# Cross-attention context: V as the stationary operand on two 64-column halves of the array, with the softmax denominators summed by ScalarE and spread by small DMAs

## The reference, cut to what matters

```python
xn = layernorm(layernorm(x)) * ln_gamma + ln_beta               # 8 batches x 256 tokens x 128
q = (xn @ w_q).reshape(B, 256, 16, 64)
k, v = split(context @ w_kv)                                    # 512 keys x 16 heads x 64
scores = einsum('bqhd,bkhd->bhqk', q * SCALE, k)
attn = softmax(scores, axis=-1)
out = einsum('bhqk,bkhd->bqhd', attn, v).reshape(B, 256, 1024)
x = x + tanh(g_xattn) * tanh(gate) * (out @ w_out + b_out)
x = x + tanh(g_ffn) * switch_ffn(layernorm(x))                  # 8 experts, 160 rows each
```

## Time and profile before

| | before |
|---|---|
| time, median of 3 (lowest to highest) | 473.65 us (472.65 to 474.98) |
| profiled execution, span from first to last instruction | 473.7 us |
| busy: PE, DVE, ACT, POOL | 439.7, 360.3, 386.4, 356.6 us |
| share of 16 DMA engines' span in the packets of SP's queue | 93.4% |
| granted TensorE clock, mean | 0.996 |
| first to last DMA transpose | 23.7 to 427.1 us |

### The profile page before, as it was taken

How to read it: one execution, slowest core, us unless ns; L and a number is a source line. 1 busy time by engine, 2 the same in 40 slices (tenths; PEclk the granted TensorE clock), 3 DMA queues, 4 the chain that set the end, 5 groups by cost and what they waited for, 6 DMA issues and landing times.

```text
span 473.7 us, 13155 instructions
## 1 busy us (share of the span) xinstructions
PE 439.7 (93%) x5096; PEld 334.0 (71%) x5096; DVE 360.3 (76%) x789; ACT 386.4 (82%) x630; POOL 356.6 (75%) x270
## 2 busy tenths in 40 slices
PE   7889799998999989999999999999999999988993
PEld 6656667776767767776777667776777677758892
DVE  4787687778877887779787796878877887785622
ACT  5889788899888988899888898899799998892330
POOL 3687686888788887888878877898878877871325
PEclk9999999999999999999999999999999999999998
DMA  5499999999999999999999999999989998996021
GB/s 167 150 177 192 206 187 175 170 181 204 188 176 188 210 194 180 192 192 192 198 189 197 189 196 191 185 200 209 190 157 185 193 180 147 159 182 137 14 67 46
DMA packets 283037, 82.10 MB, mean 173 GB/s; under 512 B 264387, under 2 KB 280435, under 8 KB 282976
## 3 DMA queue, kind: packets, MB, share of 16 engines
q1 hardware_dynamic: 281600, 77.96, 93.4%
q0 software_dynamic: 1376, 3.30, 2.2%
HBM read 10.83 MB, written 5.14 MB: 34 GB/s over the span
## 4 chain that ended last, share of the span: by engine, by line
PE 40%; DVE 20%; ACT 16%; DMA 10%; issue 8%; POOL 4%; POOLq 0%; SPq 0%; ACTq 0%; DVEq 0%
DVE MXL L903 9%; DMA PT<-PARTS 9%; ACT P L752 7%; DVE HL L890 4%; ACT HL L714 4%; PE psAB L1234 3%; PE psX L1319 3%; PE psAB L1241 3%; PE psO L1267 3%; ACT PARTS L762 3%; POOL PARTS L650 3%; PE psX L1355 3%; DVE VL L896 3%; PE psO L1269 3%; PE psO L1268 3%
## 5 line engine op out<-in xcount | busy, mean ns | idle before, releaser
L650 POOL TENSOR_TENSOR PARTS<-P,PARTS 128x1024 f16<-128x1024 f32 x125 | 267.4, 2145 | 63.5 <-ACT PARTS L762 61.8
L762 ACT ACTIVATE PARTS<-P 128x1024 f16<-128x1024 f32 x126 | 136.1, 1080 | 0.7
L752 ACT ACTIVATE P<-psAB,NB 128x512 f32<-128x512 f32 x128 | 81.6, 695 | 41.8 <-DVE NB L906 41.4
L903 DVE TENSOR_REDUCE MXL<-psAB 128x2 f32<-128x1024 f32 x64 | 78.4, 1224 | 41.4 <-PE psAB L1241 23.9
L1267 PE MATMUL psO<-VH,PT 128*128 128x65 f16 x1008 | 98.6, 194 | 8.3 <-DMA PT<-PARTS 7.7
L1267 PEld LDWEIGHTS psO<-VH,PT 128*128 128x128 f16 x1008 | 92.0, 98 | 12.0 <-DMA PT<-PARTS 8.9
L1268 PE MATMUL psO<-VL,PT 128*128 128x64 f16 x1008 | 98.5, 192 | 0.0
L1269 PE MATMUL psO<-VH,PT 128*128 128x65 f16 x1008 | 98.4, 193 | 0.0
L1268 PEld LDWEIGHTS psO<-VL,PT 128*128 128x128 f16 x1008 | 91.3, 98 | 0.5
L1269 PEld LDWEIGHTS psO<-VH,PT 128*128 128x128 f16 x1008 | 91.5, 97 | 0.0
L752 ACT ACTIVATE P<-psCD,NB 128x512 f32<-128x512 f32 x128 | 81.7, 703 | 0.1
(11 more groups left out here) (214 smaller groups left out, 871.7 us busy)
## 6 DMA issues: line engine op xcount, KB each, us to landing
ctx_raw<-in_ctx_dram SPq DMA_DIRECT2D x8, 256.0 KB, 3.7
w1s<-in_L_ffn_w_dram SPq DMA_DIRECT2D x8, 256.0 KB, 3.6
w2s<-in_L_ffn_w_dram SPq DMA_DIRECT2D x8, 256.0 KB, 4.0
PT<-PARTS SPq DMA_TRANSPOSE x126, 5.0
experts_table<-zeros POOLq DMA_DIRECT2D x2, 645.0 KB, 4.0
X<-in_x_dram SPq DMA_DIRECT2D x8, 128.0 KB, 4.2
wraw<-in_L_xattn_w_kv_dram SPq DMA_DIRECT2D x4, 256.0 KB, 5.3
out_dram<-row SPq DMA_DIRECT2D x8, 128.0 KB, 2.5
```

Source lines behind the costliest of these rows:

```text
L650: pool.tensor_tensor(PARTS[:, par, qt, 1], P32[:, par, qt], PARTS[:, par, qt, 0], ALU.subtract).then_inc(plo_done, 1)
L752: last = act.activation(P32[:, par, qt, SK * h:SK * h + SK], score_bank(qt)[:, SK * h:SK * h + SK], ACT.Exp, bias=NB[:, par, qt, h:h + 1])
L762: act.activation(PARTS[:, hp % 2, qt, 0], P32[:, hp % 2, qt], ACT.Copy).then_inc(phi_done[qt], 1)
L903: dve.tensor_reduce(MXL[:, par, qt, :, 0], score_bank(qt)[:].rearrange("p (h n) -> p h n", h=2), AX.X, ALU.max, negate=True).then_inc(max_ ...
```

## The change

V becomes the stationary operand. For each key tile and each of the three products, head 0's V (128 keys x 64) sits on the first 64 columns of the array and head 1's on the other 64, and PT moves with 256 columns (both query tiles). That makes 24 matmuls for each pair instead of 48; psO[0:64] and psO[64:128] hold the two heads' context with the queries along the row. It is already the layout of OT, so `o_transposes`, `ot_copy`, the tensor O and their semaphores go. The sums of the exponentials no longer come out of the matmul: `exps` writes them by ScalarE's accumulator output into `den`. They lie there with the queries on the partitions, while OT needs them along the row, so DVE's `recips` takes reciprocals into `rden`, SP stores these 512 numbers one by one into a DRAM buffer (`recips_store`) and loads each head's 256 numbers back into 64 partitions (`recips_load`, two DMAs). Only the last pair goes another way: a copy on POOL, two PE transposes and a copy on ACT.

```diff
+    recip_rows = nc.dram_tensor("recip_rows", (2, 2, SQ), F32).ap()
@@ sync
+            def recips_store(j):
+                par = j % 2
+                sp.wait_ge(rden_done, j + 1)
+                if j >= 2:
+                    sp.wait_ge(recips_in, 32 * (j - 1))
+                sp.dma_start(recip_rows[par].rearrange("h (t p) -> p h t", p=P), rden[:, par],
+                             allow_slow_non_contiguous=True).then_inc(recips_out, 16)
+            def recips_load(j):
+                par = j % 2
+                sp.wait_ge(recips_out, 16 * (j + 1))
+                if j >= 2:
+                    sp.wait_ge(norm_done, j - 1)
+                for h in range(2):
+                    sp.dma_start(rdenT[DH * h:DH * h + DH, par, :], recip_rows[par, h:h + 1, :].to_broadcast([DH, SQ]))\
+                        .then_inc(recips_in, 16)
...
                     if j < LAST:
-                        for qt in range(QT):
-                            transpose_parts(j, qt)
+                        transpose_parts(j, 0)
+                        recips_store(j)
+                        transpose_parts(j, 1)
+                        recips_load(j)
@@ scalar
-            def ot_copy(n, bank=psOT, pairs=1):
...
+            def recip_copy():
...
                     last = act.activation(P32[:, par, qt, SK * h:SK * h + SK], score_bank(qt)[:, SK * h:SK * h + SK],
-                                          ACT.Exp, bias=NB[:, par, qt, h:h + 1])
+                                          ACT.Exp, bias=NB[:, par, qt, h:h + 1], accum_out=den[:, par, h, qt:qt + 1])
@@ vector
+            def recips(j):
+                par = j % 2
+                dve.wait_ge(exp_done, 2 * j + 2)
+                if j >= 2:
+                    dve.wait_ge(recips_out, 16 * (j - 1))
+                dve.reciprocal(rden[:, par], den[:, par]).then_inc(rden_done, 1)
...
             def normalise_heads(b, hp):
...
-                dve.reciprocal(rden[:, hp % 2, :], sums[:, :, DH]).then_inc(rden_done, 1)
...
+                    dve.wait_ge(recips_in, 32 * (j + 1))
...
+                dve.tensor_tensor(OT[:, hp, :], psO[:, 0:SQ], rdenT[:, hp % 2, :], ALU.mult).then_inc(norm_done, 1)
...
                     row_max(b, hp, 0)
+                    if j:
+                        recips(j - 1)
@@ tensor
-                            pe.matmul(psO[:, g:g + DH + 1], phi, VH[:, kt, head, 0:DH + 1], start=first_, stop=False)
-                            pe.matmul(psO[:, g:g + DH], phi, VL[:, kt, head, :], start=False, stop=False)
-                            last = pe.matmul(psO[:, g:g + DH + 1], plo, VH[:, kt, head, 0:DH + 1], start=False,
-                                             stop=last_)
+                pt = PTL[:] if j == LAST else PT[:, par]
+                for kt in range(KT):
+                    for v, s in ((VH, 0), (VH, 1), (VL, 0)):
+                        for h in range(2):
+                            last = pe.matmul(psO[DH * h:DH * h + DH, 0:SQ], v[:, kt, 2 * hp + h, :], pt[:, :, s, h, kt, :],
+                                             start=(kt == 0 and v is VH and s == 0),
+                                             stop=(kt == KT - 1 and v is VL))
...
-            def o_transposes(n, bank=psOT, pairs=1):
...
+            def spread_recips():
```

More of the change, by code:

```diff
@@ L258, in gated_block @@
         rden_done = sem("rden_done")
+        recips_out = sem("recips_out")
+        recips_in = sem("recips_in")
+        recip_spread = sem("recip_spread")
+        recip_psum = sem("recip_psum")
+        recip_copied = sem("recip_copied")
         norm_done = sem("norm_done")
-        ot_psum = sem("ot_psum")
-        ot_done = sem("ot_done")
         proj_psum = sem("proj_psum")
@@ L731, in router_exp @@
                 last.then_inc(lexp_done, 1)
-            def ot_copy(n, bank=psOT, pairs=1):
[L735 to L742, removed]
+            def recip_copy():
+                act.wait_ge(recip_psum, 1)
+                act.wait_ge(norm_done, LAST - 1)
+                act.activation(rdenT[:, LAST % 2, :], psRT, ACT.Copy).then_inc(recip_copied, 1)
             def exps(b, hp, qt):
@@ L1070, in batch @@
                         place(B - 2)
+                        recips(LAST)
                     if hp == LOGITS_STEP and is_last(b):
@@ L1314, in project_part @@
                     wait_x((part_done, b + 1))
-                pe.wait_ge(ot_done, b * PAIRS + pairs[-1] + 1)
+                pe.wait_ge(norm_done, b * PAIRS + pairs[-1] + 1)
                 pe.wait_ge(wo_in, 16)
@@ L1318, in project_part @@
                     for pair in pairs:
-                        last = pe.matmul(bank[:, D * qt:D * qt + D], OT[:, pair * QT + qt, :], wo[:, pair, :],
+                        last = pe.matmul(bank[:, D * qt:D * qt + D], OT[:, pair, P * qt:P * qt + P], wo[:, pair, :],
                                          start=(pair == pairs[0]), stop=(pair == pairs[-1]))
@@ L1344, in project_last @@
                     for pair in pairs:
-                        last = pe.matmul(dst, OT[:, pair * QT + qt, :], wo[:, pair, :], start=(pair == pairs[0]),
+                        last = pe.matmul(dst, OT[:, pair, P * qt:P * qt + P], wo[:, pair, :], start=(pair == pairs[0]),
                                          stop=(pair == pairs[-1]))
@@ L1354, in project @@
                     for pair in range(PAIRS // 2, PAIRS):
-                        last = pe.matmul(dst, OT[:, pair * QT + qt, :], wo[:, pair, :], start=(pair == PAIRS // 2),
+                        last = pe.matmul(dst, OT[:, pair, P * qt:P * qt + P], wo[:, pair, :], start=(pair == PAIRS // 2),
                                          stop=(pair == PAIRS - 1))
@@ L1399, in batch @@
                         q_project(*next_pair(b, hp, AHEAD))
-                    if ot_pair(j) >= 0:
-                        if not ahead:
-                            pe.wait_ge(kq_done, LAST + 1)
-                            pe.wait_ge(ot_done, ot_pair(j))
-                        o_transposes(ot_pair(j))
                     if hp == RANKS_STEP and b > 1:
```

78 lines of the change are left out of this document (27 added, 51 removed).

## The result

The changed kernel takes **973.13 us** (967.79 to 974.95, 4 runs) against 474.15 us of the kernel before (472.65 to 474.98, 4 runs) on the same chip: a ratio of 2.048, 95% interval 2.042 to 2.054. The forecast was 530, with 485 to 600 as its range. The sign was right and the size was far off: 499 us were added, not 56.

What follows compares the result with a forecast made beforehand. SP's ordered DMA list was taken to bound the changed kernel, 7.4 us a pair against a period of 6.45; 62 x 0.95 = 59, less 1 for start and end, on 473.7 gave 531.7, rounded to 530 us, range 485 to 600.

Steps and rivals of the forecast that it cites:

- What bounds the kernel: SP's ordered DMA list: 5.6 us of a 6.45 us pair before, 0.85 to spare; 7.4 after the change, 0.95 over.
- The issue of the new DMAs: On SP's queue, each pair: 0.58 us for the store, 1.05 for two loads, 0.15 for further waits and steps.
- The store waits for `rden_done`: SP's store waits for DVE's reciprocals, which stand behind the next pair's first maximum: taken as 0, up to 0.3 us.
- the store's landing: SP's loads wait for it: 2.5 us against 3.1 of issues between, so wait 0; upper bound 4.6, a 1.5 us wait.
- The late-store rival: Single numbers into DRAM land as late as scattered rows, 4.6 us: 625 us, or 590 at 1 us of wait; chance 0.13.
- a sixth of 5 us: DMA packets: 512 + 128 more beside two transposes' 4,096 add at most 0.8 us a pair, 0.4 of it in spare time.
- The ring through VectorE: DVE standing at the multiplication for `recips_in` would hold up the next maximum; put at nothing.
- The column halves overlap: PE's values matmuls on two column halves run together: 1.44 us a pair, not 2.88, making PE 0.24 us a pair shorter.
- Start and end: Outside the pairs: O's last transposes and ACT copy (0.49 + 0.61 us) leave, the last loads join; counted as -1 us.
- No overlap: Rival: PE's column halves run in series, PE gets 1.2 us a pair longer, period 7.65, time 548 us; chance 0.15.
- Packets only: Rival: SP's issue time is pushed back, not spent, so only the packets' time counts: 498 us; chance 0.10.
- Faster: Rival: SP's list does not bind, PE and ACT do, 0.24 and 0.41 us less; 458 us with PE's share; chance 0.08.

Runs made afterwards that it cites:

- the loads alone: Changed kernel with only the first two pairs' stores kept; every pair's two loads stay and later ones reread those old numbers: 547.17 us, ratio 1.154.
- the run with the store alone: Changed kernel with each pair's store of 512 single numbers but without the reciprocal loads, a constant standing in rdenT: 810.78 us, ratio 1.707.
- the run without DMAs: Changed kernel without the store and two loads of the reciprocals, constants in their place except for the last pair: 483.04 us, ratio 1.017.
- the run with 16-byte runs: Changed kernel with all its DMAs, but the store writes each partition's four numbers side by side, 128 runs of 16 bytes (wrong scales): 563.09 us, ratio 1.182.

## Why the prediction was wrong in size

- **What bounds the kernel: right.** SP's ordered list had little to spare: between the issues of the kernel before lie 55.5 us, 0.89 a pair, where 0.85 and 0.15 were taken. With the loads alone its timeline has hardly a gap. What that list costs when it is full was taken too low (below).
- **The issue of the new DMAs: right in the changed kernel, too low in a full list.** 0.534 us for the store (0.58 taken), 1.09 for most pairs of loads (1.05 taken), but there SP had stood for 6.6 us (416.3 / 63) before the loads. Where it issues without a pause, two loads take 1.4 us.
- **The store waits for `rden_done`, taken as 0: right.** It waited once, 1.5 us.
- **The failed step: the store's landing.** It was taken from the row store at 2.5 us, with the scattered DMA's 4.6 us as the upper bound. It is 9.3 us, twice the bound. Runs of 512 bytes were a row for a DMA of as many runs, but no row had single numbers side by side, and that is what costs: the same 512 numbers 64 bytes apart landed in 2.9 us. The late-store rival named the place and put 4.6 us at its end, so the range ended at 600 and that rival at 625 (its case of a wait of 1 us works out to 594, not 590, and the 555 of both waits to 556; nothing rests on either).
- **A step that was missing: what the store does to others.** Late landing was priced as a wait of SP. By the run with the store alone, the store costs 328 us over the run without DMAs with nobody waiting for its landing in the same pair. Transposes behind it land in 10.3 to 11.3 us in place of 5.0. The estimate of "a sixth of 5 us" for the added packets took all packets for equally long. The ring through VectorE, put at nothing, stayed small in the changed kernel (11.4 us of waiting for the loads at the product), but it is what took the gain when the loads came a pair later.
- **The sum with the failed step mended** is the run with 16-byte runs: a period of (513.1 - 24.1) / 62.5 = 7.82 us and 563.09 us, against 7.4 and 530. SP's queue in it, us a pair between the first and the last transpose:

| | taken | 16-byte runs |
|---|---|---|
| issue of two transposes | 5.05 | 4.84 |
| issue of two loads | 1.05 | 1.44 |
| issue of the store | 0.58 | 0.64 |
| SP's other DMAs | 0.4 | 0.36 |
| between issues | 0.30 | 0.55 |

  So the loads behind other DMAs and the time between issues are the terms that were small; the transposes were not.
- **The column halves overlap: right.** The 24 value matmuls start at 202.23, and their last group of two starts 1.22 us later and lasts 0.28 (the run without DMAs, where the clock was full; columns are start, length):

```profile
202.23 0.41 PE L1277 MATMUL psO<-PT,VH 128*64 128x256 f16 x4
202.47 0.28 PE L1277 MATMUL psO<-PT,VL 128*64 128x256 f16 x2
...
203.45 0.28 PE L1277 MATMUL psO<-PT,VL 128*64 128x256 f16 x2
```

  That is 1.50 us to the end, where 24 in series at 0.12 would need 2.88. The Trainium skill, "TensorEngine Tiling (Array Packing)", section "Theoretical Speedup", gives up to 2x for such a stationary operand, and this trace agrees. But PE's busy time in the window fell from 384.05 to 380.27 (at a granted clock of 0.99 in place of 1.00), 0.06 us a pair and not 0.24: the size of that term was wrong.
- **ACT: right.** 0.08 us for each sum lies in the 0 to 0.2 taken. **DVE: right**, 424 ns for the product, 178 ns for the reciprocal.
- **Start and end, taken as -1 us: wrong.** Without the DMAs the stretch behind the last transpose's start is 49.0 us against 46.6, at a granted clock of 0.88 to 0.89 where the kernel before had 1.00 and 0.95. Without the sums as well it is 47.2. In the changed kernel it is 53.4, with the last loads in it.
- **The rivals.** No overlap fell. Packets only fell in its price, since the loads' few packets alone cost 64 us where it had 498 for everything. Faster fell even without the DMAs. Late store was the right one in kind, with its price below half of the truth.

The granted clock was 0.75 in a stretch in which PE stood waiting for `PT` in each pair. That lengthens the stretch behind each landing: the value matmuls from 312.97 took 2.77 us to the end of their last group at 315.74 where they took 1.50 at full clock (1.2 and 2.4 GHz are the two levels). So part of 14.30 us is the clock. It follows the late transposes and is not their cause: in the run with 64 bytes between the numbers, with the same DMAs in the same order, the mean is 0.93.

The Trainium skill, "DMA: Bandwidth & Descriptors", section "Specifications", says that transfers below 512 bytes are done by reading, modifying and writing. That alone would charge all the stores of 512 single numbers the same, and they differ by 402 us (973.13 and 571.35); what these runs add is that such writes land later the closer together they fall. That a read and a write stand behind each of them is not shown by any run here. The same page, section "Back-pressure in remote DMA", tells that stalled writes also stall other queues of their engine, for transfers between cores. No run here has a second queue to show that; on one core and in one queue, the transposes behind the store landed after 10.3 us.

**Left open:** the exact distance at which single writes stop holding each other up. 64 bytes are far enough (584.40), 16 bytes nearly or fully (616.66 and 571.35), 4 bytes are not; 32 and 8 were not tried. Also the last 0.3 to 0.7% of the rest, and why the order of neighbours moves 834 to 973 at 4 bytes and 617 to 571 at 16. Not tried either: issuing the store and the loads from another engine than SP, which would tell how much of the 64 us of the loads, or of the 563.09, is the length of SP's list and how much is the shared DMA engines.

## What to carry to other kernels

A DMA is not priced by its bytes or by its number of runs alone: ask whether single numbers from different places end up side by side in DRAM, and if so keep each partition's numbers together as one run or give every number 64 bytes of its own. Price a new DMA also by what it does to those that share its engines, by an upper bound that is not the largest row at hand when none of the rows has its shape. And where one queue issues in a fixed order, add up its issues first, at the lengths that they have in a full queue: here two small loads took 1.4 us a pair and not 1.05, and cost 72 us over the kernel before where the sum gave 16.

## What the hardware showed that was not expected

- 512 single numbers written side by side into 2 KB of DRAM land in 9.3 us, 128 of them into 512 bytes in 8.3, 512 with 64 bytes between them in 2.9; transposes in flight behind the dense ones land in 7.8 to 11.3 us in place of 5.0.
- VectorE's reciprocal of 128x256 numbers, read with each repeated 64 times, took 1.75 us against 0.18 for 128x4; a copy of that shape took 1.18 us, where a product of 128x256 took 0.42.
- A sum at the output of ScalarE appears as an instruction of its own of about 0.2 us, while ScalarE's busy time grew by 0.08 us for each:

```profile
L753 ACT ACTIVATION_READ_ACCUMULATOR P<-psCD,NB 128x1 f32 x128 | 28.2, 220 | 0.0
```

- Halving the array's columns between two matmul streams gave nearly the full factor of two for 256-column matmuls (1.50 us against 2.88 in series, the latter an estimate), and the kernel gained nothing from it.
